# Ranking the free edges in a graph network kernel: the scan's constant factor of one moves from SBUF to a PSUM column

## The reference, cut to what matters

```
x = x + L0_gnn(layernorm(x), src, dst)          # attention over 206250 edges, 6250 nodes, 4 heads of 64
x = x + L0_ffn(layernorm(x))                    # 8 experts, top 2
x = x + L1_gnn(layernorm(x), src, dst, weight)  # weighted sum over the same 206250 edges
x = x + L1_ffn(layernorm(x), edge_index)        # router is attention over 131072 "free" edges; 4 experts, top 2
```

## Time and profile before

| | us |
|---|---|
| median of 3 runs | 10050.34 |
| lowest, highest of the 3 | 9975.06, 10080.99 |
| the profiled execution | 10034.82 |
| its span, first to last instruction | 10033.0 |
| VectorE busy in it | 4209.3 |
| GpSimd busy in it | 5911.6 |
| TensorE matmuls busy in it | 5820.6 |

### The profile page before, as it was taken

The page is one execution under the profiler, slowest core; times in us unless marked ns, Lnnn a source line. Parts: engine busy times, 40 slices in busy tenths (PEclk is TensorE's granted clock), DMA queues, the critical chain, the costliest instruction groups (busy, mean ns, idle before and its releaser), DMA issues. The chain is left out here.

```text
span 10033.0 us, 126311 instructions
## 1 busy us (share of the span) xinstructions
PE 5820.6 (58%) x26833; PEld 4849.7 (48%) x26834; DVE 4209.3 (42%) x13437; ACT 1325.3 (13%) x3508; POOL 5911.6 (59%) x6707
## 2 busy tenths in 40 slices
PE   3777666566671499924444454455421666666693
PEld 2556555445451488822333333333321666666693
DVE  4666566566675300034444444444410333333412
ACT  0112111111110233310000000000100111111231
POOL 3666666556566466656666666666357666666335
PEclk7777777677775699966676666667755555555696
DMA  3333332222221255443333333332000000011264
GB/s 110 81 83 85 83 84 77 68 74 79 72 79 50 94 162 163 163 122 91 88 88 89 90 88 88 89 89 72 1 3 18 7 7 7 7 6 7 62 210 150
DMA packets 413320, 773.78 MB, mean 77 GB/s; under 512 B 132919, under 2 KB 238843, under 8 KB 412974
## 3 DMA queue, kind: packets, MB, share of 16 engines
q0 software_dynamic: 247360, 507.26, 19.7%
q1 hardware_dynamic: 165870, 265.54, 8.0%
HBM read 707.96 MB, written 64.40 MB: 77 GB/s over the span
## 5 line engine op out<-in xcount | busy, mean ns | idle before, releaser
L716 POOL DMA_INDIRECT g_G<-table,g_STG x3328 | 3235.3, 972 | 1941.7 <-issue 937.0
L954 PE MATMUL g_pM<-g_G,g_S 128*128 128x260 f32 (+1 forms) x6656 | 2392.5, 513 | 1466.7 <-DVE g_S L799 662.6
L954 PEld LDWEIGHTS g_pM<-g_G,g_S 128*128 128x128 f32 x6656 | 1584.0, 256 | 2097.5 <-issue 944.6
L808 DVE TENSOR_TENSOR acc<-g_pM,acc 128x260 f32 (+1 forms) x3328 | 1414.7, 425 | 1233.3 <-remote 639.6
L1377 POOL DMA_INDIRECT q_G<-table,q_STG x1072 | 1018.8, 950 | 632.0 <-issue 310.0
L590 POOL DMA_INDIRECT slots<-sort_PAIR,sort_ADDR x1024 | 1027.8, 1004 | 504.9 <-issue 312.0
L799 DVE TENSOR_SCALAR g_S<-iota,g_REL,g_WT 128x128 f32<-128x128 f32 x1664 | 595.9, 359 | 389.8 <-issue 207.0
L941 PE MATMUL g_pA<-keep,g_ST 128*128 x3328 | 498.9, 276 | 390.8 <-ACT g_ST L886 308.1
L1492 PE MATMUL q_pA<-keep,q_ST 128*128 x2144 | 476.8, 346 | 419.2 <-ACT q_ST L1456 390.4
L1492 PEld LDWEIGHTS q_pA<-keep,q_ST 128*128 128x128 f32 x2144 | 482.8, 331 | 429.9 <-issue 429.9
L941 PEld LDWEIGHTS g_pA<-keep,g_ST 128*128 128x128 f32 x3328 | 485.7, 226 | 420.2 <-issue 416.3
(11 more groups left out here) (283 smaller groups left out, 5710.5 us busy)
## 6 DMA issues: line engine op xcount, KB each, us to landing
e_W<-in_L_ffn_W SPq DMA_DIRECT2D x210, 512.0 KB
g_G<-table,g_STG POOLq DMA_INDIRECT x3328
e_W<-in_L_ffn_W SPq DMA_DIRECT2D x202, 256.0 KB
ys<-e_Y SPq DMA_DIRECT2D x206, 128.0 KB
q_G<-table,q_STG POOLq DMA_INDIRECT x1072
slots<-sort_PAIR,sort_ADDR POOLq DMA_INDIRECT x1024
rows<-t_XR SPq DMA_DIRECT2D x98, 128.0 KB, 1.7
ew_W<-in_L_ffn_W SPq DMA_DIRECT2D x8, 1024.0 KB, 7.7
```

The costliest lines, as they stand in the source:

```text
L716: pool.indirect_dma_start(G[:, r, u, :], None, table, bass.IndirectOffsetOnAxis(ap=STG[:, r, u:u + 1].bitcast(U32), axis=0)).then_inc(gath ...
L808: v.tensor_tensor(sums, pM[u % BANKS][:, 0:width], sums, ALU.add).then_inc(s["added"], 1)
L954: pe.matmul(pM[u % BANKS][:, 0:width], S[:, r, u, :], G[:, r, u, :], start=True, stop=True).then_inc(s["sum"], 1)
```

## The change

The scan's first input becomes a column of PSUM. The column is the first free one of `pF`, it is set to 1.0 once by VectorE in the first group, and the scan waits for the semaphore of that.

```diff
@@ graph_pass
     if sort is not None:
-        names += ["prep", "rank0", "dist", "eq", "scan", "scan_seen", "rank", "prefix", "base", "addr"]
+        names += ["prep", "rank0", "dist", "eq", "scan", "scan_seen", "rank", "prefix", "base", "addr", "one"]
@@
             before, totals = pAX[:, 128:128 + NB + 1], pAX[:, 256:256 + NB + 1]
+            one = pF[:, 2 * GRP * HEADS:2 * GRP * HEADS + 1]
@@ prepare
                     v.tensor_copy(KEY[:, :], sh.iota[:, 0:NB + 1]).then_inc(s["prep"], 1)
+                    v.memset(one, 1.0).then_inc(s["one"], 1)
@@ scan_block
+                v.wait_ge(s["one"], 1)
                 v.wait_ge(s["eq"], b + NB + 2)
                 v.wait_ge(s["rank"], b + 2)
-                v.tensor_tensor_scan(SCAN, sh.ones[:, 0:1].broadcast_to([P, NTF]), EQ[j], BASE[:, bass.ds(b, 1)],
+                v.tensor_tensor_scan(SCAN, one.broadcast_to([P, NTF]), EQ[j], BASE[:, bass.ds(b, 1)],
                                      ALU.mult, ALU.add).then_inc(s["scan"], 1)
```

## The result

Measured in 20 runs of either kernel, the median is 10098.2 us after the change and 10022.65 us before. The ratio is 1.0072, with a 95% interval of 1.0051 to 1.0093: the change makes the kernel slower by 0.72%, where I had forecast it faster by 0.35%. The time lies inside the range that I gave, but only because the range was wide enough for half of a rival; the direction is the wrong one.

The account below looks back on a forecast made before the run. The prediction took a ring of GpSimd gathers, VectorE steps and TensorE sums to limit the rank stage. 10034.8 - 35.5 = 9999 us profiled, other terms 0; with the median 15.5 us above, about 10015 us; range 9925 to 10130.

Parts of the forecast that it names:

- the hold: Rank stage: a gather wanting to start during a scan waits until it ends; 29 such gathers lose 35.5 us.
- Step 2: The scan's own time, 2349 ns x 50, unchanged by the PSUM input: 0, bounds 3.5 us either way.
- Step 3: New wait before the scan and the one memset: hidden, together 0, bound 2 us.
- R3: Rival, 0.14: the scan's length, output or SBUF `BASE` column causes the hold, which stays; 10050 us.
- step 1: Rank stage: the hold of 29 gathers goes and counts in full, 35.5 us; bounds 0 and 35.5.
- gait (b): Rank stage, scan hits a gather: two groups back to back, then some 5 us rest; 28 intervals, 26.3 us each.
- gait (c): Rank stage, scan falls into GpSimd's rest: VectorE waits until after the double burst; 21 intervals of 31.95 us.
- the short kind: Rank-stage intervals under 24 us; the prediction had not separated them from gait (b)'s 26.3 us each.
- R2: Rival, 0.12: rank-stage pairs go over to gait (c); all 28 cost 158 us, 10208 us; over 1% from 18.
- the mark of 650: Sign of R2: GpSimd's idle time before the rank stage's gathers (L716) above 650 us.
- R1: Rival, 0.16: without the hold the rank stage falls into the count stage's gait, 165 us less, 9885 us.
- the ring: The limiting loop: gathers of group k, VectorE's step, TensorE's sums, permission for the gathers four groups on.

Follow-up runs that it names:

- e5: The kernel after the change, unchanged, on a prompt chip (kernel before about 8410 us): 8340.82 us for 8419.26 before, ratio 0.9905.
- e1: Kernel after the change, but the scan reads SBUF again; column, memset and wait stay: 8413.77 us for 8410.99 before, ratio 1.0002.
- e3: Kernel after the change, predicated copy replaced by a product with the PSUM column, ranks not kept: 8274.96 us, ratio 0.9840 to before.
- e4: Kernel before the change, predicated copy replaced by a product with the PSUM column, ranks not kept: 8367.68 us, ratio 0.9949 to before.
- e15: Kernel after the change plus a GpSimd memset of 1100 columns in each odd rank group, late chip: 10010.51 us for 10046.63 before, ratio 0.9983.
- e10: Kernel before the change plus a GpSimd memset of 512 columns within every group, late chip: 9948.06 us for 9991.94 before, ratio 0.9938.
- e11: Kernel after the change, predicated copy split into two parts of 512 columns, on a late chip: 9951.08 us for 9991.94 before, ratio 0.9963.
- e16: Kernel after the change, predicated copy replaced by a product with the PSUM column, on a late chip: 9945.36 us, ratio 0.9899 to before.
- e9: Kernel after the change, predicated copy split into two parts of 512 columns, on a prompt chip: 8285.0 us, ratio 0.9850 to before.

## Why the prediction was wrong

**What held.** The mechanism of the hold: all 29 are gone, the busy time of the gathers fell by the 35.2 us counted, the longest gather is 2062 ns beside the predicated copy, and the mean is 986 ns (980 forecast). The copies' holds, which the prediction had put at 38 and 20.6 us, are 42 and 24.8 us before the change; no other term hung on that. Step 2, the scan's time at 0: 2350 ns for 2349. The estimate of 65 ns more for an input in PSUM, worked out from the Trainium skill (VectorE: DVE Perf Modes, the section on the TRN2 errata), is not borne out: the scan takes 2350 ns in e5 too. Step 3, wait and memset at 0: e1's ratio is 1.0002. R3 fell: no scan with its factor in PSUM held a gather in any run. The rule that it was weighed with (the Trainium skill, SBUF — State Buffer, "Who interferes with whom") agrees with e1, e3, e4 and e5: 93.5 and 94.3 us are held beside the scans that read SBUF twice (e1, e4), nothing beside those with one input in PSUM (e3, e5).

**What failed is step 1**, in the sentence that the hold's 35.5 us count in full "since the wait at 2726.18 ends while the burst is still going and so moves with the burst", and the forecast's "the gaits otherwise as they are". The gaits didn't stay. The term measured is not -35.5 but about +78 us on the rank stage's 50 intervals: 18 pairs went from gait (b) to gait (c) at some 5 us each (+92 us), 5 went to the short kind (-21 us), and the pairs that stayed in their kind are a few us longer together. This is R2, which I had at 0.12, in 18 of its 28 intervals: just the number from which I had said that it decides; that it came to 0.72% and not to 1% is due to the 5 short pairs, and to a gait (b) of 27.1 us that I had read as 26.3. Both of its signs came: 39 intervals for 21, and 684.6 us of idle ahead of gathers against the mark of 650. Against R2 I had written that the release in (b) follows the copy's hold, which stays. It does stay (34 gathers are held by it), and gait (c) came nevertheless. What went were the double bursts that begin with the odd group, 26 of them to 3: only in those does the copy's hold fall into the second half. So R1 had a part of the truth as well, that the hold allows double bursts, though only of this order. I had also taken the two gaits as fixed by where the scan falls, when in (c) the scan falls into the rest because GpSimd has been left standing: the gait decides what the scan meets, and not only the other way round.

**Was it the loss of the break?** The traces let one count how VectorE's late starts end. A late start is one that comes over 3 us after TensorE's last instruction for `pA`, after the landing of the step's rows (by their DMA packets) and after VectorE's own last instruction. The table counts them over the 100 steps of the rank stage, by where in GpSimd's burst of gathers they end:

| | late starts | behind the end of a burst | inside a burst |
|---|---|---|---|
| before | 43 | 22 | 21 |
| after | 38 | 38 | 0 |
| e15 (after, and a memset of 1.03 us in the odd groups) | 42 | 9 | 33 |
| e10 (before, and a memset of 0.54 us in all groups) | 39 | 5 | 34 |
| e11 and e16 (no long hold by the copy) | 19 and 15 | 18 and 14 | 1 and 1 |
| each of the twelve traces of prompt chips | 0 | 0 | 0 |

Before the change, 19 of the 21 that end inside a burst are even steps that come 3 to 7 us behind a gather held by the predicated copy. After it there are none, and every late start lasts until the burst is over. The memset of e15 brings them back, the gait falls to 17 intervals, and the loss disappears; 16 double bursts begin with the odd group again. In e10, with more breaks, the late starts end in the same way. That is strong support for the break. It doesn't show how long a break must be, nor that the memset acts as a break and not by shifting the ring in time.

e11 and e16 show the other half: where the copy holds no gather at the head of the even group (e16) or next to none (e11: five, 1.5 us), double bursts become rare (10 and 11 of 100 groups follow without a rest, for 38 after the change and 47 before), and gait (c) with them. My reading of the step from one kernel to the other is this: without the scan's hold the double bursts begin with the even group, with the copy's hold at their head and nothing behind it to break them. Removing both holds, or halving the copy, avoids the bursts. All of this rests on counts of single profiles, and the change itself was not run again on the late chips of the experiments, so its own comparison is that of the record.

**What stays open** is why the late chips are late. It looks as if a release reaches VectorE and GpSimd only when the stream of gathers pauses. GpSimd shows it too: in the count stage before, it rests over 1 us ahead of 90 of 98 groups, and for 81 of these the last sum that it waits for had ended before the burst in front did. Slow transfers are not the cause: from the start of a gather to its last packet 2.43 us pass before and 2.44 us in e1, at the median. But the rest of the count stage stays in e10, so either a break of 0.54 us is too short there, or it must fall after the release has been sent, or it is something else. The traces of late chips hold less than half as many semaphore records (60,710 before, 60,400 after, against 135,154 in e1), so when a release was sent can't be read from them. A sweep of the break's length and place on a late chip would tell it apart; it wasn't tried.

## What to carry to other kernels

A VectorE scan or predicated copy of 1024 columns with two tensor inputs in SBUF holds what GpSimd would start beside it, an indirect DMA or a copy of its own. Put a constant input into PSUM, or cut the instruction until it fits inside one gather, and measure the removal of all such holds together, not only of one. In a ring in which several engines wait for one another, count a removed stall at nothing until it is known what the stall kept apart, and read how many rounds of the ring are in which gait rather than the mean round. And a gain measured on one chip may be a loss on another: here the same edit was -0.95% where the ring was bound by GpSimd and +0.72% where its engines stood waiting for one another.

## What was unexpected of the hardware

The same program takes about 8415 us on some chips and about 10020 us on others, a difference far larger than any edit of this study. Of the 1620 us between the spans of e1 and before, 1240 lie in the three passes that gather rows by edge (2243, 2101 and 1355 us from first to last gather in e1, 2806, 2456 and 1677 before): 10.2 against 12.8 us a group in the count stage, with a gather at 955 ns on both. The granted TensorE clock differs too (0.738 against 0.692 on the mean of the span), but TensorE is busy 5627.2 us in e1 and 5820.6 us before, which is 193 us of the 1620.

A held gather ends 0.76 us after the scan that held it (2.93 us from 1800.08 in e1) and 0.80 us after the copy (2.06 us from 2046.81 after the change), and one that has started beforehand isn't disturbed (e9). A plain copy of GpSimd is held likewise, but ends with VectorE's operation (0.45 us from 1506.15 in e9), and in e1 such copies cost nearly as much (41.5 us) as the held gathers that take their place in e5 (54.4 us).
